# Identity products on TensorE in the waits of the mixer's last chunks, of the seam and of the last token tiles

## The reference

```python
x = x + mamba_mixer(layernorm(x))   # 64 heads of 64 in 8 groups, state of 128, causal convolution of 4 taps
x = x + swiglu(layernorm(x))        # 4-bit weights, dequantized; inner width 1376
x = x + attention(layernorm(x))     # softmax(q k / 4) v over a token's own 16 x 16 dims, 32 heads, 8 for k and v
x = x + moe_lora(layernorm(x))      # x W^T + b, and rank-16 LoRA of the top 2 of 8 experts
```

## Time and profile before

| | before |
|---|---|
| median of the runs | 1378.74 us |
| the profiled execution | 1378.88 us |
| its span, first to last instruction | 1377.1 us |
| PE busy | 1292.6 us (94%) |
| DVE busy | 921.6 us (67%) |
| ACT, POOL busy | 677.4 us (49%), 550.4 us (40%) |
| granted TensorE clock, mean | 0.975 of full speed |

### The profile page before, as it was taken

How to read it: one execution, slowest core, us unless ns; L and a number is a source line. 1 busy time by engine, 2 the same in 40 slices (tenths; PEclk the granted TensorE clock), 3 DMA queues, 4 the chain that set the end, 5 groups by cost and what they waited for, 6 DMA issues and landing times. The chain is left out here.

```text
span 1377.1 us, 20772 instructions
## 1 busy us (share of the span) xinstructions
PE 1292.6 (94%) x6262; PEld 1009.9 (73%) x6262; DVE 921.6 (67%) x1762; ACT 677.4 (49%) x1055; POOL 550.4 (40%) x557
## 2 busy tenths in 40 slices
PE   5699999999999999999999999999889999879986
PEld 4577877877887787788788778877666666667764
DVE  5876677667667666766766676677665455368995
ACT  3465565566556556656655665664523322222220
POOL 2245335444533534443453444334532334333330
PEclk9899999999999999999999999999989999999996
DMA  4211011011101101100200110010103222131200
GB/s 150 59 47 33 1 62 34 17 33 47 31 1 62 31 16 32 51 28 1 65 29 16 32 59 19 1 36 1 39 16 107 84 76 80 54 94 29 58 16 23
DMA packets 44248, 57.61 MB, mean 42 GB/s; under 512 B 10182, under 2 KB 21156, under 8 KB 43922
## 3 DMA queue, kind: packets, MB, share of 16 engines
q1 hardware_dynamic: 44178, 56.84, 13.5%
HBM read 49.87 MB, written 6.96 MB: 41 GB/s over the span
## 5 line engine op out<-in xcount | busy, mean ns | idle before, releaser
L413 POOL TENSOR_TENSOR x_w<-xs,head_g 128x512 f32<-128x512 f32 x56 | 58.6, 1047 | 280.2 <-ACT xs L522 255.5
L615 DVE SCALAR_TENSOR_TENSOR conv<-p_tile,conv_taps,conv 128x511 f32<-128x511 f32 x189 | 140.8, 745 | 27.6 <-ACT conv L489 17.3
L432 POOL TENSOR_TENSOR y<-y,x_d 128x512 f32<-128x512 f32 x56 | 72.0, 1285 | 170.7 <-DVE y L754 170.7
L726 DVE TENSOR_TENSOR em<-em,p_gb 128x512 f32<-128x512 f32 x128 | 82.2, 684 | 73.0 <-ACT em L528 73.0
L494 ACT ACTIVATE xbc<-conv 128x512 f32<-128x512 f32 x96 | 60.4, 630 | 134.2 <-DVE conv L623 77.6
L1026 PEld LDWEIGHTS p_y<-x_dt,em 128*128 128x128 f32 x896 | 108.6, 192 | 16.1 <-issue 13.0
L615 DVE SCALAR_TENSOR_TENSOR conv<-p_d,conv_taps,conv 128x511 f32<-128x511 f32 (+2 forms) x99 | 73.9, 747 | 68.9 <-ACT conv L489 65.0
L93 PE MATMUL p_tile<-xn_hi,wc_hi 128*128 128x512 f32 x252 | 110.9, 440 | 2.7 <-DVE halo L619 2.7
L93 PE MATMUL p_gate<-wr_hi,xn_hi 128*128 128x512 f32 x256 | 107.0, 418 | 1.1 <-ACT gate L510 1.1
L1026 PE MATMUL p_y<-x_dt,em 128*128 128x64 f32 x896 | 106.1, 271 | 1.0 <-DVE x_res L643 1.0
L93 PE MATMUL p_y<-wr_hi,zt_hi 128*128 128x512 f32 x256 | 103.4, 404 | 1.6 <-ACT zt_hi L498 1.6
(11 more groups left out here) (336 smaller groups left out, 3301.0 us busy)
## 6 DMA issues: line engine op xcount, KB each, us to landing
w_raw<-w SPq DMA_DIRECT2D x112, 256.0 KB, 2.8
q_words<-q SPq DMA_DIRECT2D x33, 256.0 KB, 2.6
h_ring<-h_lo_rows SPq DMA_DIRECT2D x6, 704.0 KB, 5.0
h_lo_rows<-h_rest SPq DMA_DIRECT2D x11, 256.0 KB, 2.0
x_res<-x SPq DMA_DIRECT2D x8, 256.0 KB, 4.5
out<-out_t SPq DMA_DIRECT2D x8, 256.0 KB, 2.1
h_lo_rows<-h_rest SPq DMA_DIRECT2D x11, 128.0 KB, 1.8
decay_lhs<-cum_parts SPq DMA_DIRECT2D x64, 6.0 KB
```

The source lines that it names most:

```text
L413: pool.tensor_tensor(by_head(x_w[:]), by_head(xs[:, c % 2, :]), heads(DTW, c), ALU.mult)\
L432: pool.tensor_tensor(y[:, c % 2, :], y[:, c % 2, :], x_d[:], ALU.add).then_inc(s_txd, 1)
L615: ve.scalar_tensor_tensor(out=conv[:, s, sh:], in0=p[:, 0:HALF - sh], scalar=conv_w[:, bass.ds(g, 1), j, tap], in1=conv[:, s, sh:], op0=AL ...
L726: ve.tensor_tensor(m, m, gm.unsqueeze(1).broadcast_to([P, HG // 2, P]), ALU.mult)\
```

## The change

A new function writes n products of the identity with itself, full float32, 128 x 128, into a bank that nobody reads at that time; their results are never used. It is called in seven stretches of the program, 70 products in all, each time behind a wait that makes sure that the bank has been read:

```diff
+def keep_clock(pe, bank, ident, n):
+
+    for _ in range(n):
+        pe.matmul(bank[:, 0:P], ident[:], ident[:], start=True, stop=True)
...
                 mm.then_inc(s_xt, 1)
+                if last and c > CH:
+                    pe.wait_ge(s_t, g * (NC - 1) + c - 1)
+                    keep_clock(pe, p_in, ident, 5)
                 if not first:
                     z_transpose(n - 1)
...
                     pe.wait_ge(*lo_count(g, WT - 1))
+                if last and c > CH:
+                    pe.wait_ge(s_res, n - 1)
+                    keep_clock(pe, p_y, ident, 7)
                 if not first:
                     out_product(n - 1)
...
         up.spread(pe, 0, 1, 1)
+        pe.wait_ge(s_t, LAST - G + 1)
+        keep_clock(pe, p_in, ident, 6)
         z_transpose(LAST)
...
                 mm.then_inc(s_dl, 1)
+            if i in (NC, NC + 1):
+                pe.wait_ge(v_add, NC)
+                keep_clock(pe, p_a, ident, 16 if i == NC else 12)
             if live(c):
                 pe.wait_ge(v_n3, c + 1)
```

## The result

| | before | after |
|---|---|---|
| median of 16 runs | 1379.84 us | 1376.72 us |
| lowest, highest | 1378.01, 1382.82 | 1374.99, 1379.33 |
| the profiled execution, its span | 1378.88, 1377.1 us | 1375.94, 1374.2 us |
| mean granted clock | 0.975 | 0.987 |

A forecast was written before the change was run, and what follows sets the result against it. PE and DVE take turns in chunks 5 and 6; PE's waits and half clock cost time elsewhere, and PE bounds the end. Terms 3.2 - 1.9 - 2.4 - 0.7 - 3.0 = -4.8 us gave 1374.2 us, range 1371.5 to 1379.4.

The forecast's parts named there:

- the sevens in chunks 5 and 6: 7 products ahead of the out product in each chunk, where PE does not wait: nothing hides them, +3.2 us.
- the price: One float32 identity product on PE: 0.23 us at full clock, estimated 0.42 us at half.
- chunk 7 and the seam: Sevens and six fill PE's waits and keep the clock full: -1.9 us in chunk 7, -2.4 at the seam.
- steps 8 and 9: Token tiles: the 16 fit in PE's wait, -0.7 us; the 12 start at half clock but restore it, -3.0 us.
- The reason given for the half clock: Step 9: with step 8 at full clock, PE stands nearly idle until hw_lo, so the clock falls before the twelve.
- The fives: 5 products ahead of z's transposes, three times: they fit in PE's waits, cost 0 (0 to +0.1 us each).
- Rival A: Seam not saved, the six products run at half clock: +1.1 us in place of -2.4, 1377.6 us; chance 0.22.
- B: Step 9's twelve come at half clock and do not bring it back: +2.3 us for -3.0, 1379.4 us; chance 0.12.
- C: Identity products do not count as work for the clock anywhere: +8.4 us, 1387.3 us; chance 0.08.
- D: The seven in chunks 5 and 6 are hidden, DVE or ACT giving the time back: 1370.9 us; chance 0.08.
- the prediction doubted that they keep the clock: Seam: 1.1 us of thin spread products and eight of 64 columns ahead of the six may not keep the clock.

The follow-up runs named there:

- e1: The changed kernel without the 7 products ahead of the out product in chunks 5 and 6 (chunk 7 keeps them): 1372.38 us, ratio to before 0.995.
- e2: The kernel before with nothing but the 7 products ahead of the out product in chunks 5 and 6: 1382.51 us, ratio to before 1.0029.
- e4: The kernel before with only the 16 and 12 products of the token tiles: 1377.50 us, ratio to before 0.998.
- e3: The kernel before with only the products of chunk 7 (5 and 7) and of the seam (6): 1377.25 us, ratio to before 0.9985.
- e5: The kernel before with only the 5 products ahead of z's transposes in chunks 5 and 6: 1379.40 us, ratio to before 1.0002.
- e6: As e4, but step 9's fill is 3 products ahead of hw's transpose, 12 ahead of L1808's third matmul, 11 ahead of the rows' transposes: 1376.39 us.
- e7: e1 with each product of the identity replaced by two transposes of the identity: 1372.39 us, ratio to before 0.9953.
- e10: e1 without the 6 products at the seam: 1373.48 us, ratio to before 0.9961.
- e8: e1 with the token-tile fill of e6: 1372.26 us, ratio to before 0.9946.
- e9: e8 with 3 more products behind the rows' transposes in steps 8 and 9: 1370.50 us, ratio to before 0.9939.

## Why the prediction was right and wrong

**Right: the sevens in chunks 5 and 6.** Forecast +3.2, in the profile +3.1, by the times of e1 and e2 3.4 to 4.3. They stand behind the gate product, where PE does not wait, and DVE's list behind the out product has no slack.

**Right: the price.** 0.21 to 0.24 us a product at full clock (1.48 us for the seven of chunk 5, 1.44 for the six of the seam), 0.42 at half as estimated (e4).

**Right in the mechanism: chunk 7 and the seam.** DVE's h_rest is what comes late next, and the row transpose waits for DVE. B fell by 4.4 us from profile to profile, forecast 4.3.

**Right: steps 8 and 9.** DVE's last rows are ready 0.75 us earlier, counted from the start of D (forecast 0.7). The twelve begin at half the clock, take 4.0 us, delay the rows by 1.4 us (forecast 1.7), and router and base product run at full. D fell by 4.1 us, forecast 3.7. The reason given for the half clock is not borne out: step 8 was not at full clock, its base product took 4.5 us and not 3 (the clock fell at 1348.4), and in before, with a slower step 8, the clock also fell, at 1359.3, behind the same wait of 3.16 us for hw_lo.

**Wrong: the size of the term for chunk 7 and the seam.** The step that failed is -1.9 - 2.4 = -4.3 us. It took what one execution of before lost there as what each loses, and let the six hold the clock each time. e3, which has only these products, measured 2.1 us (0.8 to 3.3). The profiles show both parts. Over the profiles, B without fill is 22.76, 21.11, 21.09, 21.54 and 21.10 (before, e2, e4, e5, e6), mean 21.5: the profile of before was the worst of five by 1.2 us. With fill it is 18.40, 19.49, 19.50, 19.30, 18.39 and 18.39, mean 18.9, since the seam falls in three of six. So chunk 7 and the seam give 2.6 us and not 4.3; by the times of e3, 2.1.

The token tiles gave less too, as far as the profiles tell. D without fill is 51.57, 51.01, 50.88 and 51.00 (before, e2, e3, e5), mean 51.1; with the sixteen and twelve 47.49, 47.41, 50.12, 47.37 and 48.36 (after, e1, e4, e7, e10), mean 48.2: 3.0 us and not 3.7, or 3.4 without the long execution of e4; e4's time, 2.8 us (1.5 to 3.9), does not exclude 3.7. 3.1 - 2.6 - 3.0 = -2.5 us, where the 16 runs say -2.8 to -3.1. The fives may add 0.5 (A is 27.15, 27.88, 28.67 and 27.16 in before, e3, e4 and e6, without fives and sevens in chunks 5 and 6, mean 27.7), but e5's time does not show it.

How far this sum can be trusted, the same profiles tell. C, in which no kernel differs from before by an instruction, lies between 296.4 and 299.5 us. From before to after A, B and D change by 3.1 - 4.4 - 4.1 = -5.4 us, but the span by -2.9: C is 1.0 us longer, and z's transposes in chunk 5 begin 1.45 us later, at 980.21 against 978.76, behind instructions that are the same in both. In every other profile they begin later than in before, too (979.07 to 980.82). So one profile against another does not tell a term to a microsecond. The times don't close the sum either: e2, e3, e4 and e5, each with one part, add up to 4.0 - 2.1 - 2.8 + 0.3 = -0.6 us by the ratios, against -2.8 for the whole. Each is uncertain by some 1.2 us, so that may be noise; whether the parts help each other is not shown.

**Rival A** (the seam is not saved) happened in part. The six ran at half in three of the six profiles that have them, but B was then 1.0 us longer than where the clock held, not the 3.5 of the rival, and still 1.2 shorter than in e10 without them. It had 0.22 as if it held for all or none. **B** happened in part in e4, where the clock came back at 1364.1 and fell again at 1367.5. Rivals **C** and **D** fell: the clock comes back among products of the identity (1362.1 in after), and nothing hides the sevens.

What stays open is why the clock fell at the seam, 0.4 to 0.5 us into six products back to back, in e1, e3 and e7 and not in after, e8 and e9. The lists of e1 and e8 are the same there. In all six the spreads and the products of 64 columns stand ahead, of which the prediction doubted that they keep the clock; no run puts fuller work in their place.

## What to carry to other kernels

Fill only where the profile shows PE waiting, place by place: of these 70 products the 14 in chunks 5 and 6 stood where it did not wait, and cost about 4 of the 7 us that the others gave. Where a loss depends on the granted clock, read it from several executions before it goes into a sum; stretches of a profile in which nothing was changed (C above) show how far to trust one. And after a fill look for the next idle stretch: in step 9 the clock fell in the 3.2 us of idle time ahead of the twelve, and a clock kept through step 9's waits (e6) fell in the product behind it.

## What the runs showed of the hardware that was not expected

The granted clock of the same instructions differs between executions: the 16 of the changed kernel have means of 0.980 to 0.987, and before and e4, whose mixers are the same, differ by place: in chunk 7, 0.76 in before and 1.00 in e4 over the same 14 us, in chunk 5 the reverse (1.00 and 0.73 over 4 us). It can fall while PE is busy without a gap (e3, at 1021.5), behind a stretch of short waits and narrow products; in the unfilled chunk 7 of before it fell at 1007.7, where no wait of PE that had ended since chunk 5 was longer than 1.34 us. And transposes of the identity bring it back as products do (e7, at 1358.3), with 1372.39 us against the 1372.38 of e1.
